# One-hots of two attention layers from a product of bit codes, with a run of unread products at the fourth group

## The reference

```python
e = jax.nn.leaky_relu(xl[src] + xr[dst], NEG_SLOPE)
logits = jnp.einsum('ehc,hc->eh', e, att)
m = jax.ops.segment_max(logits, dst, num_segments=N)
ex = jnp.exp(logits - m[dst])
denom = jax.ops.segment_sum(ex, dst, num_segments=N)
alpha = ex / denom[dst]
msg = xl[src] * alpha[..., None]
out = jax.ops.segment_sum(msg, dst, num_segments=N)
```

## Time and profile before

| | us |
|---|---|
| median of 3 runs | 6715.57 |
| lowest and highest | 6712.33, 6718.6 |
| the profiled execution | 6720.51 |
| its span | 6718.6 |
| TensorE (PE) busy | 4849.3 (72%) |
| VectorE (DVE) busy | 4075.3 (61%) |
| ScalarE (ACT) busy | 2302.0 (34%) |
| GpSimd (POOL) busy | 4529.0 (67%) |

### The profile page before, as it was taken

How to read it: one execution, slowest core, us unless ns; L and a number is a source line. 1 busy time by engine, 2 the same in 40 slices (tenths; PEclk the granted TensorE clock), 3 DMA queues, 4 the chain that set the end, 5 groups by cost and what they waited for, 6 DMA issues and landing times. The chain is left out here.

```text
span 6718.6 us, 98108 instructions
## 1 busy us (share of the span) xinstructions
PE 4849.3 (72%) x22735; PEld 3497.7 (52%) x22735; DVE 4075.3 (61%) x13068; ACT 2302.0 (34%) x5676; POOL 4529.0 (67%) x4354
## 2 busy tenths in 40 slices
PE   3677765237777666543886996666666799999998
PEld 2344443236664444332775996555555455555555
DVE  7898985589976676334887445444444644344343
ACT  4344444259953333333995003222222400000000
POOL 1777777778857777777886661777777177375473
PEclk9555555569965555555997998777777799999999
DMA  5988865457644444333444884655555299999998
GB/s 202 298 301 287 278 188 147 114 100 142 141 80 108 106 106 104 81 80 48 76 76 105 290 283 146 186 161 159 161 159 157 67 304 305 295 304 297 300 304 255
DMA packets 915215, 1226.12 MB, mean 182 GB/s; under 512 B 248092, under 2 KB 652720, under 8 KB 901674
## 3 DMA queue, kind: packets, MB, share of 16 engines
q1 hardware_dynamic: 593614, 879.21, 40.8%
q0 software_dynamic: 206208, 217.12, 16.7%
q10 hardware_dynamic: 114828, 123.48, 5.6%
HBM read 981.30 MB, written 239.21 MB: 182 GB/s over the span
## 5 line engine op out<-in xcount | busy, mean ns | idle before, releaser
L1180 POOL DMA_INDIRECT ACC<-table,TABS x1760 | 1665.7, 946 | 609.2 <-issue 609.2
L1495 POOL DMA_INDIRECT BUF<-table,TABS x840 | 797.6, 949 | 589.8 <-issue 244.7
L1261 POOL DMA_INDIRECT adjacency<-TABS x600 | 966.8, 1611 | 301.8 <-issue 264.7
L1801 POOL DMA_INDIRECT TABS<-table,SPOT_SRC x836 | 789.3, 944 | 317.9 <-issue 317.9
L1983 PE MATMUL picked<-BUF,G 128*128 x2368 | 596.1, 433 | 448.6 <-DVE ACC L2008 402.3
L1983 PEld LDWEIGHTS picked<-BUF,G 128*128 128x128 f32 x2368 | 526.2, 327 | 690.7 <-issue 690.7
L2379 PE MATMUL asum<-BUF 128*128 128x144 f32 x3520 | 561.6, 305 | 166.3 <-DVE BUF L2357 163.4
L1991 DVE TENSOR_TENSOR picked<-picked,ACC 128x512 f32<-128x512 f32 (+1 forms) x440 | 247.6, 563 | 574.1 <-DMA ACC<-table,TABS 503.0
L1824 PE MATMUL pre<-wmat,BUF 128*128 128x128 f32 x1672 | 321.2, 352 | 358.5 <-DVE BUF L1850 346.2
L2379 PEld LDWEIGHTS asum<-BUF 128*128 128x128 f32 x3520 | 476.8, 197 | 197.2 <-issue 184.3
L2325 ACT ACTIVATE BUF<-iota_row,TABS 128x128 f32<-128x128 f32 x1760 | 555.2, 386 | 22.6 <-PEq L98 22.6
(11 more groups left out here) (449 smaller groups left out, 9783.9 us busy)
## 6 DMA issues: line engine op xcount, KB each, us to landing
TABS<-adjacency SPq DMA_DIRECT2D x272, 512.0 KB
BUF<-in_edge_pair SPq DMA_DIRECT2D x836, 128.0 KB
BUF<-adjacency SPq DMA_DIRECT2D x102, 1024.0 KB
BUF<-adjacency SPq DMA_DIRECT2D x204, 512.0 KB
adjacency<-zeros ACTq DMA_DIRECT2D x44, 1792.0 KB
G<-adjacency SPq DMA_DIRECT2D x136, 512.0 KB
kept<-ACC SPq DMA_DIRECT2D x220, 272.0 KB, 3.7
G<-kept SPq DMA_DIRECT2D x220, 272.0 KB
```

Of the source, the lines that this page charges most:

```text
L1180: po.indirect_dma_start(rows[:, slot, j, 0:width], None, tab, bass.IndirectOffsetOnAxis(ap=SRC[:, q * GT + j:q * GT + j + 1], axis=0)).the ...
L1261: po.indirect_dma_start(adj_flat, bass.IndirectOffsetOnAxis(ap=PLACE[:, k:k + 1], axis=0), TOTAL[:, k:k + 1], None, compute_op=ALU.add).th ...
L1495: po.indirect_dma_start(R[:, q % deep_ring, j, :], None, table, bass.IndirectOffsetOnAxis(ap=SRC[:, k:k + 1], axis=0)).then_inc(S(f"gather ...
L1801: po.indirect_dma_start(R[:, g % RD, j, :], None, table, bass.IndirectOffsetOnAxis(ap=SPOT_SRC[:, k:k + 1], axis=0)).then_inc(S(f"gathered ...
```

## The change

In `gat_sums`, for both layers:

- The four `Abs` of `hots` and the relu of `exps` go. A load of the group's codes (`fetch_codes`, 32 rows of 256 bytes, on SP's queue, between `fetch_max` and `fetch_rows`) and one bf16 product on TensorE (`meet`, 32 rows by 512 columns, after `turn_max`) come, and `hots` becomes one relu from PSUM. The order on ACT turns from `hots`, `exps` to `exps`, `hots`. The two new PSUM tiles are `meets`.
- At the fourth group (`q == RUN_UP`) eight fp32 products of 384 columns are put out ahead of the group's own. They go to columns of `mcol` that nobody reads.

```diff
+RUN_UP, RUN_UP_LONG = 3, 8
...
+                def fetch_codes(q, slot, turn):
+
+                    wait(sp, S("met"), q - CD + 1)
+                    settle(sp, "sync")
+                    sp.dma_start(coded[:, q % CD, :], code_d[q * GT:(q + 1) * GT].rearrange("t b e -> (t b) e")
+                                 ).then_inc(S(f"codes{q % CD}"), 16)
+
+                def meet(q, slot, turn):
+
+                    pe.wait_ge(S(f"codes{q % CD}"), 16 * (q // CD + 1))
+                    wait(pe, S("hot"), q - 1)
+                    pe.matmul(meets[slot % 2][:, :, :].rearrange("p t d -> p (t d)"), coded[:, q % CD, :],
+                              COLUMNS[0:CODE_ROWS, :, :].rearrange("p t d -> p (t d)"), start=True, stop=True
+                              ).then_inc(S("met"), 1)
+
                 def hots(q, slot, turn):
 
-
+                    ac.wait_ge(S("met"), q + 1)
                     wait(ac, S("summed"), q - RING + 1)
-                    for j in range(GT):
-                        ac.activation(HOT[:, slot, j, :], iota_row[:, :], ACT.Abs, scale=-1.0,
-                                      bias=LOCAL[:, bass.ds(q * GT + j, 1)]).then_inc(S("gap"), 1)
+                    ac.activation(HOT[:, slot], meets[slot % 2][:, :, :], ACT.Relu).then_inc(S("hot"), 1)
 
                 def exps(q, slot, turn):
                     ac.wait_ge(S("dif"), q + 1)
                     ac.activation(RHS[:, slot, :, W:W + H], DIF[:, slot], ACT.Exp).then_inc(S("exp"), 1)
-                    ac.wait_ge(S("gap"), (q + 1) * GT)
-                    ac.activation(HOT[:, slot], HOT[:, slot], ACT.Relu, scale=-1.0, bias=1.0
-                                  ).then_inc(S("hot"), 1)
...
+                    if q == RUN_UP:
+                        for _ in range(RUN_UP_LONG):
+                            pe.matmul(mcol[0][:, P:4 * P], ident[:, :], X[:, 0:3, :].rearrange("p b d -> p (b d)"),
+                                      start=True, stop=True)
                     wait(pe, S("added"), (q - 1) * GT)
...
-                pipeline(nc, [(fetch_max, 0), (fetch_rows, 1), (turn_max, 2), (ve_step(less_max), 2),
+                pipeline(nc, [(fetch_max, 0), (fetch_codes, 0), (fetch_rows, 1), (turn_max, 2), (meet, 2),
+                              (ve_step(less_max), 2),
                               (ve_step(first_rows), 3), (ve_step(first_max), 2), (ve_step(last_rows), 3),
                               (ve_step(weight_column), 2), (add, 5),
-                              (flush, 0), (hots, 2), (exps, 2), (products, 4)])
+                              (flush, 0), (exps, 2), (hots, 2), (products, 4)])
```

More of the change, by code:

```diff
@@ L2288, in gat_sums @@
             whole, R, LOGIT = ring(W, H)
+            coded = CODES[:, :, :].rearrange("p r e -> p (r e)")[0:CODE_ROWS, 0:CD * P].rearrange(
+                "p (r e) -> p r e", r=CD)
             with ExitStack() as ps:
+                meets = [psum(ps, f"meets{i}", [P, GT, P]) for i in range(2)]
                 mcol = [psum(ps, f"mcol{i}", [P, 4 * P]) for i in range(2)]
```

## The result

The changed kernel takes 6939.7 us (median of 4 runs, 6937.4 to 6947.3) against 6715.6: a ratio of 1.0333 (1.032 to 1.0347), 224 us slower. I had forecast 6755 and a range to 6795. The direction was right, the size was not.

A forecast was written before the change was run, and what follows sets the result against it. VectorE was taken to bound layer 1 and ACT layer 2, with SP becoming layer 1's bound after the change. Layer 1's +50.5 and layer 2's -11 gave +39.5 us: median 6755, range 6718 to 6795.

The forecast's parts named there:

- SP as the bound of layer 1 at the full clock: Layer 1: the codes load as SP's sixth issue makes its group 2.27 us, above VectorE's 2.01; +45 us after -2.
- the 14 that I scaled over: Layer 1, SP's queue: its own stalls, some 13 us in 213 groups, scaled to 14 us and added in full.
- the 16 runs that I call longer than 1.28 us: Layer 1 before the change, SP's queue: 16 slow runs of four maxima loads between 1440 and 1890 us, some 13 us.
- TensorE's 1.75 us in layer 2: Layer 2: with the new product TensorE needs 1.75 us a group, nearly tied with VectorE's 1.71; layer 385 us, -16.5.
- -11: Layer 2 in total: -16.5 us from the loop and +5.5 for the unread products.
- the -16.5 of the loop: Layer 2's saving without the unread products: 220 groups at 1.75 us, 385 us.
- The floor that I named: Layer 2's end: the barrier also waits for POOL's last merge, so more than 20 us can't be had.
- the sum's layer 1: Layer 1 in total: +47 for SP, -2 for its lead, +5.5 for the unread products, +50.5 us.
- meet a clock that is up already: Start of each layer: work itself raises the clock, so the eight unread products only cost, +5.5 us per layer.
- the +39.5 that I had: Whole kernel: layer 1's +50.5 and layer 2's -11 us together; this forecast had chance 0.74.
- Rival B: Layer 1's clock: half-clock groups cost TensorE 3.3 us; at 60% of groups some +125 us, about 6830; chance 0.06.
- Rival A: Layer 1: SP's sixth issue hides and VectorE's rate stays; -25 us in all, 6691; chance 0.13.
- Rival C: Layer 2: `meet` waiting for codes and relu gives 1.9 us a group, 418 us; about 6788; chance 0.07.

The follow-up runs named there:

- e10: Changed kernel with the codes product over 128 rows and no unread products, codes still on SP's queue: 6760.3 us, ratio 1.0074 to the kernel before.
- e7: Changed kernel with the codes product over 128 rows instead of 32, the added right-operand rows zero, unread products kept: 6764.1 us.
- e9: Changed kernel with the codes product over 128 rows, no unread products, codes loaded by ACT's queue: 6690.9 us, ratio 0.9967 to the kernel before.
- e11: Kernel before with the change in layer 2 alone, codes product over 128 rows, no unread products, codes on SP: 6697.9 us, ratio 0.9979.
- e1: Changed kernel without the eight unread products, 32-row codes product kept: 7249.2 us, beside 6724.6 for the kernel before.
- e5: Kernel before with one more unread bf16 product of 32 rows per group of layer 1: 6951.4 us, beside 6724.6.
- e6: Kernel before with one more unread bf16 product of 128 rows per group of layer 1: 6706.3 us, beside 6724.6.
- e4: Changed kernel with the eight unread products again at every 16th group of layer 1, 32-row product, codes on SP: 6885.6 us.
- e3: Changed kernel with the load of the codes moved from SP's queue to ACT's, 32-row product and unread products kept: 6850.5 us.

## Why the prediction was wrong, point by point

- **SP as the bound of layer 1 at the full clock: right, and too small.** 2.27 us a group was forecast; in the short stretch at full clock the kept rows of the changed kernel start at 1461.96 and 1464.24, 2.28 apart:

```profile
1461.96 0.35 SPq L2312 DMA_DIRECT2D G<-kept  x1
1462.42 1.28 SPq L2306 DMA_DIRECT2D BUF<-heads  x4
1463.82 0.31 SPq L2328 DMA_DIRECT2D CODES<-codes  x1
1464.24 0.45 SPq L2312 DMA_DIRECT2D G<-kept  x1
```

  With the clock repaired (e10), SP's sixth issue costs layer 1 +57.9 us where I had +45: 2.38 us a group. The stalls of the queue took about 19 us, not the 14 that I scaled over: the runs of maxima lost 9.6, and 18 issues of kept rows were long, by 9.5 us in all, where the kernel before has two at most. My count was off as well: the 16 runs that I call longer than 1.28 us are those over 1.6; with the smaller ones the kernel before has 35, and 17 us. In the changed kernel itself none of it shows, as TensorE's 3.21 us hide SP's 2.27.
- **TensorE's 1.75 us in layer 2: right.** Products of two groups that follow each other there, in the changed kernel:

```profile
3413.88 1.25 PE L2397 MATMUL asum<-BUF 128*128 128x144 f32 x8
...
3415.60 1.25 PE L2397 MATMUL asum<-BUF 128*128 128x144 f32 x8
```

  They start 1.72 us apart, with TensorE busy 388 of 396 us. With the half-clock start and the unread products (8.06 us, begun at half clock) the layer gave -5.5 instead of -11; in e7, where only the height of the product differs, it gave -11.9. Where these go (e9, e10, e11) it gave 16 to 18, near the -16.5 of the loop. The floor that I named is nearly reached: in e9 POOL's last merge ends at 3535.5 and the last addition at 3538.8.

```profile
3533.90 1.58 POOL L1262 DMA_INDIRECT adjacency<-TABS  x1 [0.31 <-issue]
```

```profile
3538.57 0.23 DVE L1211 TENSOR_TENSOR ACC<-ACC,asum 128x67 f32 x1 [0.49 <-DVE ACC L1211]
```

- **The step that failed: the sum's layer 1 stands at the full clock, +50.5 us, and has no term for the clock; it measured +226.9, at TensorE's 3.21 us a group at half clock instead of SP's 2.27.** It rests on taking for granted that the clock comes up by itself, at the start, where the unread products "meet a clock that is up already", and behind every pause as in the kernel before. I read the rise some 7 us into the products and said that it comes "by work that is now greater". The added work doesn't count like the other: with it the clock stayed at half for three groups, and (e1) for 440. The windows of e5 and e6 show that the number of rows of one product decides, with type, columns and place the same. And e7, the changed kernel with that alone mended, is the kernel that my sum describes: 6764.1 us beside 6724.6, one run each, which is the +39.5 that I had. That it fits to the digit is luck: its layers gave +63.1 and -11.9 where I had +50.5 and -11, and the other stages 12 less.
- **Rival B had the right place and the right price of a group** (3.3 us, measured 3.21) and got 0.06, since I measured it by TensorE's busy share, 77% as before. Busy share was the wrong gauge: 99.5% busy went with half clock here. It also let the clock be down for 60% of the groups; it was down for some 200 of 220. The Trainium skill (TensorE: Matmul & The Clock Gate, Part 1: The HAM clock gate) says that the gate is set by how busy TensorE has been; read as busy time, the windows of e1 and e5 disagree for thin products, and the measurement decides.
- Rival A (the sixth issue hides) fell with e10. The Trainium skill's 50 ns of dispatch (DMA: Bandwidth & Descriptors, Anatomy of one DMA), given for GpSimd's kind, doesn't hold for SP's queue, where the rows show 0.31. Rival C (a new wait in layer 2) fell: the pace there is TensorE's own.

What stays open: how many rows between 32 and 128 are enough, and how large a share of thin work a loop may hold. In e7 the 96 added rows of the right operand are zero, so it isn't the values on that side; the rows of the left operand, which is loaded as weights, were always added together with them, so which of the two sides counts is not shown, and what lay in the added rows of the left one was not set. What makes some of SP's issues long was not tried.

## What to carry to other kernels

When TensorE gets a new instruction, ask how many rows it reads, not only how many columns it streams: a product of 32 rows in a loop that otherwise holds its clock can pin it to 1.2 GHz, and filling the other rows with zeros gave some 175 us back here (6939.7 to 6764.1). When a clock dips and returns in a profile, don't take the return for granted when you add to the loop: try it with the addition alone, as in e5. And an engine that the page doesn't list as busy, SP's queue, can be the tightest resource: lay its issues out over one period before giving it another; ACT's queue took this load at next to no cost (layer 2 385.1 us in e9, 383.6 in e10). The version with both repairs (e9) is the fastest of the study, 0.33% under the kernel before.

## What the runs showed that I had not expected

- TensorE busy for 699 of 702 us at a granted clock of 0.50 (e1), without ever rising.
- One unread bf16 product of 128 rows by 512 columns per group shortened layer 1 from 465.9 to 456.4 us (e6), one of 32 by 512 lengthened it to 702.4 (e5).
- In the loops with the thin product the full clock was lost behind pauses of 0.71 us (e4, layer 2), 0.86 (e3) and 1.65 (the changed kernel), and in e4 at 1661 us behind three in a row of 0.46 to 0.52; the kernel before lost it after one of 1.31 us and got it back.
- A loop with the thin product kept a clock that was up: layer 2 of the changed kernel ran from its unread products to its end at the full clock, TensorE hardly pausing (0.98 over the layer).
